# A table of places in time is changed around the last batch: three attention steps earlier on TensorE, the last routing later

## The reference

```python
x = x + _L0_xattn_ref(_layernorm(x), k, bias, ctx, ctx, 8)     # long convolution over the feature axis, 8 heads
x = x + _L0_ffn_ref(_layernorm(x), W, ..., A, B, gates)        # dense product + top-2 of 16 low-rank experts
x = x + _L1_xattn_ref(_layernorm(x), ctx, wq, wkv, wp, ...)    # attention, 16 heads; int8 fake-quantised input of wq and of wp
x = x + _L1_ffn_ref(_layernorm(x), router_w, ..., shared_*)    # top-4 of 32 experts, plus one shared expert
```

```python
def _qdq(x):
    s = jnp.maximum(jnp.max(jnp.abs(x), axis=-1, keepdims=True) / 127.0, 1e-08)
    return jnp.clip(jnp.round(x / s), -127.0, 127.0) * s
...
out = _qdq(o) @ _qdq(wp).T + bp
```

## Time and profile before

| | |
|---|---|
| median of 3 runs | 669.77 us (669.5 to 671.5) |
| profiled execution, its own time | 667.12 us |
| its span, first to last instruction | 665.0 us |
| mean granted TensorE clock | 0.969 |
| PE busy | 583.7 us, 88% |
| DVE busy | 439.8 us, 66% |
| ACT busy | 385.2 us, 58% |
| POOL busy | 372.8 us, 56% |
| chain that ended last | PE 65%, DVE 14%, POOL 7%, ACT 6%, issue 5%, DMA 2% |

### The profile page before, as it was taken

The page is one execution under the profiler, slowest core; times in us unless marked ns, Lnnn a source line. Parts: engine busy times, 40 slices in busy tenths (PEclk is TensorE's granted clock), DMA queues, the critical chain, the costliest instruction groups (busy, mean ns, idle before and its releaser), DMA issues.

```text
span 665.0 us, 14801 instructions
## 1 busy us (share of the span) xinstructions
PE 583.7 (88%) x4205; PEld 469.8 (71%) x4205; DVE 439.8 (66%) x1449; ACT 385.2 (58%) x1133; POOL 372.8 (56%) x527
## 2 busy tenths in 40 slices
PE   1588899999998899997999789877689999999995
PEld 1487877787777687786787557655467788788873
DVE  1646656677766977666866675658395778867663
ACT  2002366756677656786656895675444666666661
POOL 7847847548357357389653542635147556565552
PEclk9999999999999999999999997989599999999999
DMA  7999999999999999323234593788654655555897
GB/s 259 282 146 336 335 334 334 334 334 318 321 314 321 316 322 314 94 81 106 90 98 135 179 325 118 221 276 300 203 156 144 185 161 160 152 152 161 244 404 271
DMA packets 129741, 155.17 MB, mean 233 GB/s; under 512 B 15264, under 2 KB 116768, under 8 KB 129408
## 3 DMA queue, kind: packets, MB, share of 16 engines
q1 hardware_dynamic: 111536, 122.63, 62.2%
q0 software_dynamic: 7632, 20.98, 8.4%
q10 hardware_dynamic: 10496, 10.62, 5.1%
HBM read 54.06 MB, written 100.28 MB: 232 GB/s over the span
## 4 chain that ended last, share of the span: by engine, by line
PE 65%; DVE 14%; POOL 7%; ACT 6%; issue 5%; DMA 2%; ACTq 0%; SPq 0%; POOLq 0%; DVEq 0%
PE ps L410 11%; PE pc L673 11%; PE pS L368 6%; PE pS L653 4%; POOL arena L1427 4%; PE ps L455 3%; PE ps L639 3%; PE po L624 2%; PE ps L482 2%; PE ps L508 2%; PE ps L516 2%; PE ps L585 2%; PE ps L499 2%; PE ps L495 1%; PE po L400 1%
## 5 line engine op out<-in xcount | busy, mean ns | idle before, releaser
L673 PE MATMUL pc<-arena,tk 128*128 128x128 f32 x768 | 107.6, 293 | 13.3 <-POOL arena L1427 7.3
L673 PEld LDWEIGHTS pc<-arena,tk 128*128 128x128 f32 x768 | 95.9, 200 | 25.4 <-issue 13.2
L410 PE MATMUL ps<-arena,work 128*128 x380 | 99.8, 386 | 1.4 <-ACT work L1181 1.4
L1427 POOL TENSOR_TENSOR arena<-arena 128x512 f32<-128x512 f32 x64 | 90.4, 1426 | 19.0 <-ACT arena L1227 18.8
L1441 POOL DMA_INDIRECT expert_rows<-stage,ixl x64 | 63.9, 998 | 37.7 <-DVE ixl L1062 19.5
L1294 ACT ACTIVATE work<-pS,work 128x128 f32<-128x128 f32 x256 | 72.4, 368 | 4.5 <-DVE work L964 4.5
L410 PEld LDWEIGHTS ps<-arena,work 128*128 128x128 f32 x380 | 65.9, 194 | 7.1 <-issue 1.8
L1171 ACT ACTIVATE tk<-work 128x128 f32<-128x128 f32 x95 | 29.4, 310 | 60.3 <-DVE work L751 55.2
L368 PE MATMUL pS<-arena,tk 128*128 x190 | 60.0, 398 | 3.5 <-ACT tk L1176 3.4
L751 DVE TENSOR_SCALAR work<-ps 128x256 f32<-128x256 f32 x95 | 40.1, 422 | 33.2 <-PE ps L410 32.6
L964 DVE TENSOR_REDUCE work<-pS 128x4 f32<-128x512 f32 x64 | 43.8, 685 | 26.4 <-PE pS L653 26.4
(11 more groups left out here) (324 smaller groups left out, 1455.9 us busy)
## 6 DMA issues: line engine op xcount, KB each, us to landing
expert_rows<-stage SPq DMA_DIRECT2D x32, 2080.0 KB, 21.6
arena<-in_w SPq DMA_DIRECT2D x16, 768.0 KB, 7.2
work<-expert_rows SPq DMA_DIRECT2D x87, 128.5 KB
stage<-xn_rows SPq DMA_DIRECT2D x64, 130.0 KB, 2.9
xn_rows<-xnD ACTq DMA_DIRECT2D x16, 512.0 KB, 7.9
arena<-y_rows SPq DMA_DIRECT2D x12, 512.0 KB
tk<-in_tk SPq DMA_DIRECT2D x1, 2048.0 KB, 9.6
work<-y_rows SPq DMA_DIRECT2D x4, 512.0 KB, 10.1
```

The source lines that it names most:

```text
L410: i = pe.matmul(p[U * k:U * k + U, 0:256], xgT[n % 3][:, 128 * c + U * k:128 * c + U * k + U], arena[:, 256 * c:][:, bass.ds(e, 256)], sta ...
L673: i = pe.matmul(pv, tk[:, h, 128 * d:128 * d + 128], kvv[:, ci, :, :].rearrange("p b (i h j) -> p (b i) h j", i=8, h=8)[:, :, hl, :], star ...
L1427: pool.tensor_tensor(kv[kk % 4][:, c, half, :].rearrange("p (i h j) -> p i h j", h=8, i=8), i0, i1, ALU.mult).then_inc(s_kv, 1)
```

## The change

Only places in the order change, and nothing of what is computed. `oP` moves two ticks earlier for every batch. `oiP` and `op` move 9 and 13 ticks earlier for the last batch only (1157 in place of 1166 and 1170), by a helper `per_but_last`. All places of the last routing but `st`, which has no step in the last group, move later: `ra` by 14 ticks, the others by 10, which is one tile.

```diff
-LAST = {"ra": -3, "rd": 4, "re": 12, "top": 21, "mb": 23, "rk": 41, "cum": 42, "list": 47, "st": 0}
+LAST = {"ra": 11, "rd": 14, "re": 22, "top": 31, "mb": 33, "rk": 51, "cum": 52, "list": 57, "st": 0}
...
+def per_but_last(t, first, last):
+    return [b for b in range(NB) if (first if b < NB - 1 else last) + BASE[b] == t]
...
-            "S": 998, "tabE": 3078, "tab": LOOP + 96, "wordE": 3112, "word": LOOP + 134, "gu2": LOOP + 118, "dn2": LOOP + 133, "conv": 430, "oP": 1138}
+            "S": 998, "tabE": 3078, "tab": LOOP + 96, "wordE": 3112, "word": LOOP + 134, "gu2": LOOP + 118, "dn2": LOOP + 133, "conv": 430, "oP": 1136}
...
-                for b in per(t, T_PE["oiP"]):
+                for b in per_but_last(t, T_PE["oiP"], 1157):
-                for b in per(t, T_PE["op"]):
+                for b in per_but_last(t, T_PE["op"], 1157):
```

## The result

| | before | after |
|---|---|---|
| median of 11 runs each, same comparison | 671.50 us (667.7 to 674.1) | 676.70 us (672.7 to 678.9) |
| ratio | | 1.0092, 95% interval 1.0067 to 1.0116 |
| profiled execution, its span | 667.12, 665.0 us | 677.92, 675.7 us |
| mean granted clock in it | 0.969 | 0.960 |

The change makes the kernel slower, by 0.67 to 1.16%, that is 4.5 to 7.8 us: 5.2 by the two medians, 6.2 by the ratio. The kernel before itself came out at 671.5 us with eleven runs; the three that I built on, 669.77, are among them. Ratios, means and clocks leave out two runs that are more than 1.5% above the shortest of their kernel, one of h2 and one of the kernel before beside e1 to e6.

What follows compares the result with a forecast made beforehand. PE, busy 88%, bounds the tile loop; before it, DVE's `oi` of batch 14 sets the pace. Terms 0.2 + 1.1 + 2.2 + 1.2 = +4.7 us on the 669.77 median gave 674.5 us, range 669.8 to 676.8.

Steps and rivals of the forecast that it cites:

- part three: Last routing later: loop starts 1.0 us sooner, but `top` and L1118 come later; +1.2 us, bounds -1.0 and +2.0.
- the base: Starting time to which the summed terms were added: the kernel before's median, 669.77 us, not its profiled execution's 667.1.
- The signs that I named: Checks in batches 14, 15 and loop start: `acc` waits 1.4 us, L1136 over 2, L410 3.3 and `top` 9 after L566.
- Part one: `oP` ahead of the shared `dn`, batches 13 to 15: +0.2 us, then +1.1 for `oi`, and a 0.23 gain in batch 15.
- the hole of batch 15: PE's idle time after ACT's copy L1301: `oP` runs there at 461.7, `dn` is not later, `oi` saves 0.23 us.
- Part two: Batch 15's `oiP` and `op` ahead of L610 and `gu`: `xC` then waits for `gu`; +2.2 us, ends +0.5 and +2.5.
- the term of 2.2: Delay of batch 15's `xC`, 472.0 in place of 469.75, with `gu` at half clock: +2.2 us taken.
- the one from `top` to L1118: DVE's stretch in the loop's first tiles: 7.21 us shrinks to 6.5, as one 0.93 us tile step moves ahead of `top`.
- The full clock over the `gu`: Rival, batch 15: PE stays at 2.4 GHz until `op`, so `xC` costs only +0.5; sum +3.0, 672.8 us; chance 0.20.
- DVE's delay is absorbed: Rival: hidden slack in batch 14's chain and PE's early loop start cancel the costs; 669.8 us; chance 0.12.
- the loop's start decides: Rival, first tiles: PE leads and the full clock holds, so the kernel gets 2.4 us faster, 667.4 us; chance 0.12.

Runs made afterwards that it cites:

- h2: Kernel after with DVE's `xC` of batch 15 ahead of the small-transpose copies and `sc`, plus a register operation on SP's last four waits; ratio 1.0061 to the kernel before.
- e1: Kernel before with only `oP` moved ahead of the shared `dn` in every batch; ratio 0.9997 to the kernel before.
- e6: Kernel after with DVE's `xC` of batch 15 ahead of the small-transpose copies and `sc`; ratio 1.0026 to the kernel before, in a slower comparison.
- g3: Kernel before with only `oP` ahead of the shared `dn` in every batch, plus a register operation on SP's last four waits; ratio 0.9983 to the kernel before.
- e2: Kernel before with only `oiP` and `op` of batch 15 moved ahead of the small transposes and `gu`; ratio 1.0033 to the kernel before.
- g4: Kernel before with only batch 15's `oiP` and `op` ahead of `gu`, plus a register operation on SP's last four waits; ratio 1.0035 to the kernel before.
- g5: Kernel before with only the last routing moved later, plus a register operation on SP's last four waits; ratio 1.0048 to the kernel before.
- f7: Kernel after with 12, 4, 12 and 4 unread transposes filling PE's gaps in the last batch; ratio 1.0040 to the kernel before.
- f10: Kernel after with `re` at tick 12 in place of 22, giving three table loads in place of four; ratio 1.0063 to the kernel before.
- e3: Kernel before with only the last routing moved later; ratio 1.0020 to the kernel before, in a slower comparison.
- g1: Kernel before with `oP` first for the last batch only, its `oiP`, `op` and `xC` ahead, and unread transposes in PE's gaps; ratio 0.9987 to the kernel before.
- f8: Kernel before with `oP` first for the last batch only, its `oiP` and `op` ahead of `gu`, and `xC` ahead on DVE; ratio 0.9994 to the kernel before.
- f0: Kernel after measured again, with only a register operation added to each of SP's last four waits; ratio 1.0100 to the kernel before.

## Why the prediction was wrong where it was

- **Direction: right; the size: too small in three places.** The whole is slower, by some 6 us against my 4.7. The steps that failed are the term of part three (1.2, and it takes 1.93), the granted clock between batches 14 and 15, which I put at nothing (+1.8 in both profiles of the kernel after), and the base (1.7). Stage by stage the profile after has +0.0 to the copy of batch 14, +2.8 to that of batch 15, +1.7 to the router's product and +1.9 to L1122, 6.5 in all, where I had 0.2, 1.1, 2.2 and 1.2. The signs that I named came, one of them just short: `acc` waits 1.53 us for `dn` (I had said 1.4), L1140 1.96 ("over 2"), `xC` does not wait for `op`, L410 at +3.24 (3.3), `top` at +9.10 (9.2).
- **The base: wrong by 1.7 us.** I added the sum to a median of three runs, 669.77. The same kernel has 671.5 in the comparison that gave the result, and 669.8, 670.3 and 670.6 in three later ones. The profiled execution, 667.1, was a short one: at a clock of 0.969 the line gives 668.9. I had said that its distance to the median lay in no stage that I could see. The clock line accounts for 1.1 of its distance to 670.0; the other 1.8 are not placed.
- **Part one: right up to the router's product.** +1.1 for batch 14 was +0.97, +0.2 for batch 13 was 0.0, and in g3 and e1 the delay reaches the router's product (+0.95 and +0.93). The whole runs of g3 and e1 show +0.5 and +0.6 at equal clock, which tells it neither from 1.0 nor well from zero. Wrong was the hole of batch 15: I had `oP` at 461.7, 0.15 us behind ACT's copy. It starts 0.93 us behind the copy's end in the kernel after, since its bank is read by the `acc` of the `dn` before it until then. The kernel before has this `acc` at 462.08 for 0.41 us, so its rows, with the order of the banks, could have told. `oi` still came sooner than forecast (3.20 us behind the start of the copy in place of 3.74, where I had given 0.23), with `dn` at full clock (0.60 us in place of 0.96).
- **Part two: right in the mechanism, a little dear.** From the quantisation to `xC` my count makes 5.95 us (466.05 to 472.0) and 5.76 were measured; counted from ACT's copy, as the term of 2.2 is, it is +1.75, since `oi` gained more than I gave it. The wait for the `gu` stands in part two alone too (6.00 us in e2 and g4), so it does not need part one.
- **Part three: mis-sized, 1.2 for 1.93.** Start, `top` and the tile step in between were within 0.1 us. The step that failed is the one from `top` to L1118: I took off the 0.93 us of the moved tile and gave 0.2 back for the ranks, 6.5 in place of 7.21. It takes 7.20. The ranks on PE stand behind a tile product (493.41) ahead of which PE idles 1.58 us for an ACT copy behind the fourth table load (491.31 to 492.59), and behind L372 (495.58, 1.04 for ACT), whose copy follows a tanh that waits 1.67 us for a tile step of DVE behind `top`. So `cum` waits 1.26 us for PE, where it waited 0.36. A table load took its 1.28 us and no more: the one ahead of the root ends at 491.02, and the root's activation begins at 491.03. The drain that the Trainium skill (ScalarE: Activation LUTs, "What ACT_TABLE_LOAD costs") adds to a load is again not to be seen. By g5 the whole price is 2.0 us in the stages and 2.7 +-0.25 at equal clock.
- **The rivals.** The full clock over the `gu` did not come with the three parts together (2.07 us in both profiles), though the clock held until the output product; it came in one of the two profiles of part one alone, and in f7 with the gaps filled. "DVE's delay is absorbed" and "the loop's start decides" are refuted by g4 and g5.

**What stays open.** At equal clock the parts alone make 0.5 + 2.1 + 2.7 = 5.3 +-0.6 us and the whole 6.2 +-0.35, by the means 3.6 +-1.3 and 6.6 +-0.9. So the runs do not show clearly that the whole costs more than its parts. What brings the fall of the clock between batches 14 and 15 is open. It makes the stage some 1.8 us longer (21.0 us against 19.2 in f10 and h2, which have the same lists up to there), but f10 and h2 had lost 1.2 us one stage earlier (25.1 us in place of 23.9). It is not bound to part one: e2, e3, g1, g4 and g5 have such a fall without part one, and e6, f10 and h2 have part one without it. With no fall in it the stage is 18.23 us without part one (the kernel before) and 19.20 with it (f10): the 0.97 of `oi`. In the comparisons where the kernel before was slower it is 18.56 (f8) and 19.47 (e6).

## What to carry to other kernels

A product that runs beside another engine's work is free only there. Before moving work ahead of it, look what stands in the waiting engine's list between the product and the step that matters, and move that too (`xC` ahead of the small copies took the stage from 5.76 to 2.40 us). For each step moved later, follow every engine to the end of the step's consumers, not to the first. A step moved ahead also needs its bank: look who reads it last. And compare stages from anchor to anchor over several executions, and neighbouring stages together, before one stage of one profile is believed: a fall of the clock that only moves makes one stage shorter and the next longer.

## What the runs showed of the hardware

- The mean granted clock of a run explains most of its time here: 0.34 us for each 0.001, and 84% of the variance of 86 runs of one kernel. The runs of the kernel after alone have 0.957 to 0.975. And where the falls lie differs between profiles with the same lists up to there: behind batch 14's copy the kernel after and f0 have one of some 6 us, f10 and h2 none.
- Transposes that nobody reads, put where PE would wait, raised the mean clock from 0.9648 to 0.9743 and took 3 to 4 us off the kernel after. They are not free: in g1 8 of them, 1.97 us with the clock low, stand ahead of the transposes of the last normalised rows, which ACT had ready at 475.57 and PE took at 477.62.
- The kernel before took 684.7 and 682.2 us in two comparisons and 669.8 to 671.5 in the others, at nearly the same mean clock (0.966 and 0.968 against 0.965 to 0.966). The record has one chip number for the comparison with 682.2 and for two of those near 670. In the profiles of e3 and f8 from there, the way from ACT's copy of batch 13 to that of batch 14 takes 26.7 us in place of 23.9. In e3 DVE has one long wait in it, put down to no engine of the core (waits by engine and line, from 418 to 447: total, times, longest); in f8 its longest there is 3.8 us for PE's `gu`, which is 3.0 in the kernel before:

```profile
DVE tk L983 <- remote: 6.0, 1, 6.0
```

What it is, no run here tells.
